# A recurrent block and two feed-forward nets on one core: the second net's down product by columns of tokens, brought back by VectorE and DMAs

## The chip, the core and the metric

The kernel runs on one core of one Trainium2 chip. Time is what the device takes for one execution, in microseconds (us). Before the change the median of three runs is 583.81 us (583.77 to 584.46).

The core has a matrix engine (TensorE, PE in the profile), a vector engine (VectorE, DVE), a scalar engine (ScalarE, ACT), a general engine (GpSimd, POOL) and a queue that here only issues DMAs (SyncE, SP). Each engine runs its own instructions in order and waits on semaphores for the others.

## What is computed

Per batch row of 1024 tokens and 256 features (four rows, so 4096 tokens), in f32, cut to what matters:

```
t   = rmsnorm(x) ;  xb = conv4(t @ Wx) ;  a, i = gates(xb @ Wa, xb @ Wi)
h   = scan(a, sqrt(1 - a*a) * i * xb) ;  h1 = x + (h * gelu(t @ Wy)) @ Wo
u   = rmsnorm(h1)
ffn = (gelu(u @ Wg) * (u @ Wu)) @ Wd                    # first FFN, inner width 1024
x1  = layernorm(x + h1 + ffn)
out = layernorm(x1 + relu(x1 @ W1 + b1) @ W2 + b2)      # second FFN, inner width 1024
```

## The kernel before

**Precision.** Every matrix operand is held as a sum of two rounded parts (`_hi`, `_lo`), and each product is three matmuls: hi by hi, hi by lo, lo by hi. The low parts are made by VectorE (`hidden_lo`, `gate_lo`), the high ones by ScalarE or GpSimd.

**Tiles.** The 4096 tokens are eight chunks of 512 (`CHUNKS`), four tiles of 128 each (`TT`). The inner width of an FFN is eight blocks of 128 (`KH`). A unit is one block of one chunk: 64 units for each FFN.

**Two ways to multiply.** `product` keeps 128x128 of a weight in the array and streams 512 tokens; its sums stand with features on the partitions. `product_by_tokens` keeps 128 tokens in the array and streams 256 columns of a weight; its sums stand with tokens on the partitions, as the row-wise LayerNorm and the output want them. The up products take the first way, both down products the second. A down step is one block of the inner width for one chunk: `down(r)` in the first FFN, `mlp_down(w)` in the second, each four token tiles by three matmuls. The second FFN's down sums of a chunk build up over eight steps in the PSUM banks `SECOND` and `SECOND + 1`.

**Transposes by blocks.** For most chunks a 512x256 matrix is transposed without TensorE: VectorE transposes blocks of 32x32 inside the partitions (STREAM_TRANSPOSE), and DMAs of 32 partitions each carry the blocks to other partitions. `move_x1` does this for x1 with 16 DMAs, `move_t` and `move_u` for t and u with 12 on SyncE's queue and 8 on SyncE's plus 4 on ScalarE's.

**Order.** It is written out by hand. `round_of(r)` on each engine is one round; eight rounds are a period p (m is the round within it). Round r does gate and up of unit r, down of unit r - 1, and in the steady state the up step of unit w = r - 11 of the second FFN and `mlp_down(w - 1)`; the recurrent block of chunk n = p + 1 is spread over rounds 0 to 7. So in period p the first FFN is at chunk p, and chunk s = p - 2 ends its second FFN: its last down step is at the end of round 3. VectorE then adds the sums to the rows at the start of round 4 (`second_sum`), takes statistics at the start of round 6 and normalises in round 7. SyncE's queue is one fixed list: loads, `move_x1`, `move_t`, `move_u`, `store_out`, chunk after chunk. The last chunk's second FFN (`step_up`, `step_down`) is written apart.

**Buffers the change touches.** `normed` holds u for its transpose, later the blocks of x1. `h1[c % 2]` holds h1 of chunk c, and after `add_x_h1` x + h1, until `first_sum(c)` has added it to the first FFN's sums. `rows[c % 2]` holds x1, then x1 + b2, then the output rows.

Of the kernel before, what the change touches and what calls it, by code (L numbers as in the profile page):

```python
# [8 lines left out]
ALU = mybir.AluOpType  # L9
# [19 lines left out]
def griffin_mlp_kernel(nc, x, norm1_w, Wx, Wy, conv_w, conv_b, Wi, Wa, lam, Wo, norm2_w, Wg, Wu, Wd,  # L29
# [14 lines left out]
    with ctx:  # L44
# [3 lines left out]
        def sem(name):  # L48
            return ctx.enter_context(nc.semaphore(name))
# [193 lines left out]
        MOVES = len(ALL_BLOCKS) * DMA  # L243
        OFF_MOVES = len(OFF_DIAGONAL) * DMA

        def by_blocks(c):
            return 1 <= c < CHUNKS - 1

# [37 lines left out]
        tT_done = sem("tT_done")  # L286
        t_blocks_ready = sem("t_blocks_ready")
        t_blocks_moved = sem("t_blocks_moved")
        first_tT_ready = [sem(f"first_tT_ready{q}") for q in range(PAIRS)]
        second_tT_ready = [sem(f"second_tT{k}_ready") for k in range(KD)]  # L290
        half_wx_done = sem("half_wx_done")
# [90 lines left out]
        def _(sync):  # L382
# [27 lines left out]
            def move_x1(c):  # L410
                sync.wait_ge(x1_blocks_ready, KD * c)
                for i, j in ALL_BLOCKS:
                    move_block(sync, flat(normed), flat(gy), x1_blocks_moved, i, j)

            def move_u(c):

                sync.wait_ge(u_blocks_ready, KD * (c - BLOCKWISE + 1))
                for i, j in OFF_DIAGONAL[ACT_MOVES:]:
                    move_block(sync, flat(u_blocks), flat(u_raw), u_blocks_moved, i, j)
# [19 lines left out]
            for c in range(2, CHUNKS):  # L439

                if c == 2:
                    sync.wait_ge(first_xh_ready, PAIRS)
                else:
                    sync.wait_ge(xh_ready, 2 * (c - 2))
                load_x(c)
                if c == 2:
                    sync.wait_ge(lo_split["d"], pieces["d"])
                    load_w("2")
                if c >= 4:
                    move_x1(c - 3)  # L450
                if c >= BLOCKWISE:
                    move_t(c)
                if c >= 4:
                    move_u(c - 1)
                    store_out(c - 4)
            for c in range(CHUNKS - 4, LAST - 1):
                move_x1(c + 1)
                if c + 3 < LAST:
                    move_u(c + 3)
                store_out(c)  # L460
# [11 lines left out]
        def _(pe):  # L472
# [11 lines left out]
            def product_by_tokens(dst, n, k, hi, lo, start, stop):  # L484

                nc.tensor.matmul(dst, hi, w_hi[n][:, k, :], start=start, stop=False, skip_group_check=True)  # L486
                nc.tensor.matmul(dst, hi, w_lo[n][:, k, :], start=False, stop=False, skip_group_check=True)  # L487
                return nc.tensor.matmul(dst, lo, w_hi[n][:, k, :], start=False, stop=stop, skip_group_check=True)  # L488

            def transposed(src, done, bank=MIX):  # L490
                for f in range(KD):
# [23 lines left out]
            def half_bank(bank, tt):  # L515
                return psum[bank + tt // 2][:, (tt % 2) * D:(tt % 2 + 1) * D]

            def toks(tt):
                return slice(tt * P, (tt + 1) * P)
# [264 lines left out]
            def mlp_down(w):  # L784
                c, m = divmod(w, KH)
                pe.wait_ge(hid_lo_ready, w + 1)
                if m == 0 and c >= 1:
                    pe.wait_ge(s2_ready, 2 * c)
                for tt in range(TT):
                    last = product_by_tokens(half_bank(SECOND, tt), "2", m, hid_hi[:, w % SLOTS, toks(tt)],  # L790
                                             hid_lo[:, w % SLOTS, toks(tt)], m == 0 and tt % 2 == 0, m == KH - 1)
                last.then_inc(e_done, 1)

            def units(r):
# [575 lines left out]
        def _(dve):  # L1370
# [182 lines left out]

            def add_mix(c, q, bank=MIX):
                dve.wait_ge(wo_done, 2 * c + q + 1)
                nc.vector.tensor_tensor(pair_of(h1[c % 2], q), psum[bank + q][:, :], pair_of(xs[c % 2], q),
                                        ALU.add).then_inc(h1_ready, 1)

# [27 lines left out]
            def first_sum(c):  # L1586
# [7 lines left out]
                for q in range(PAIRS):  # L1594
                    nc.vector.tensor_tensor(pair_of(rows[c % 2], q), psum[DOWN + q][:, :], pair_of(h1[c % 2], q),
                                            ALU.add).then_inc(s1_ready, 1)

            def second_sum(c):
                dve.wait_ge(e_done, 8 * c + 8)
                dve.wait_ge(b2_added, 4 * c + 4)  # L1600
                for q in range(PAIRS):
                    total = pair_of(rows[c % 2], q)
                    nc.vector.tensor_tensor(total, psum[SECOND + q][:, :], total,
                                            ALU.add).then_inc(s2_ready, 1)

            def gate_times_up(r):
                dve.wait_ge(gelu_ready, r + 1)
# [112 lines left out]
            def round_of(r):  # L1720
# [13 lines left out]
                    if m == 3 and not mixing:  # L1734
                        split_x1_lo(f)
                if m == 4 and second:
                    second_sum(s)
                if m == 5 and mixing and p == 1:
                    scan_both(n)
                if m == (7 if p == 1 else 6) and mixing:  # L1740
# [33 lines left out]
                        hy_lo(n)  # L1774
                if units(r):
                    gate_lo(r)
                if m == 3 and mixing and first and by_blocks(f):
                    split_x1_lo(f)
                if m == 7 and mixing and p >= 2 and n < LAST:
# [143 lines left out]
        def _(pool):  # L1923
# [46 lines left out]
            def norm_u(c):  # L1970
# [5 lines left out]
                if by_blocks(c - 2):  # L1976

                    pool.wait_ge(x1_blocks_moved, MOVES * (c - 2))
                pool.wait_ge(rms2_rstd, h1_squares(c))
                for tt in range(TT):  # L1980
                    nc.gpsimd.tensor_scalar(normed[:, tt, :], h1[c % 2][:, tt, :], rstd2[:, tt:tt + 1], 0.0,
# [158 lines left out]
```

## Time and profile before

| | before |
|---|---|
| median of three runs | 583.81 us |
| profiled execution, its own time | 584.09 us |
| its span (first to last instruction) | 582.3 us |
| TensorE busy | 575.0 us, 99% |
| VectorE busy | 410.3 us, 70% |
| ScalarE busy | 313.9 us, 54% |
| GpSimd busy | 208.5 us, 36% |

A busy matmul is not one that sets the pace: records of neighbouring matmuls overlap, since they are pipelined. What one costs is the distance from its start to the next one's start. One period (69 us) lies between like instructions of neighbouring chunks in the steady state.

### The profile page before, as it was taken

The numbers are of one execution on the slowest core, as the hardware profiler recorded it, in microseconds if no ns is written. First come the engines' busy times: TensorE is split into PE (matmuls) and PEld (weight loads), VectorE is DVE, ScalarE is ACT, GpSimd is POOL, SyncE is SP. The second block draws the span as 40 slices with busy tenths as digits, with TensorE's granted clock in tenths as the row PEclk, the third lists the DMA queues.
The fourth block names the chain that finished last, engine by engine and source line by source line (L and its number), as shares of the span: only waits on it lengthen the run. The fifth ranks groups of instructions, "written<-read, shape, count | busy, mean of one in ns | idle before, by whom it ended". The sixth has DMA issues, their size and how long they took to land.

```text
span 582.3 us, 9342 instructions
## 1 busy us (share of the span) xinstructions
PE 575.0 (99%) x3409; PEld 508.5 (87%) x3409; DVE 410.3 (70%) x737; ACT 313.9 (54%) x600; POOL 208.5 (36%) x318
## 2 busy tenths in 40 slices
PE   8999999999999999999999999999999999999996
PEld 7768888898888988889888988889898898888996
DVE  5889858867747779486885869658795757454665
ACT  6977765844538336483446643575443833232453
POOL 2111335274242543327333354523624043132130
PEclk9999999999999999999999999999999999999999
DMA  7410310011100131002210012100110001100111
GB/s 271 155 37 8 103 36 2 2 27 37 30 7 1 33 95 29 10 1 53 77 37 0 12 43 77 34 1 23 51 33 23 2 1 37 36 1 1 37 37 38
DMA packets 29438, 22.38 MB, mean 38 GB/s; under 512 B 3896, under 2 KB 28624, under 8 KB 29392
## 3 DMA queue, kind: packets, MB, share of 16 engines
q1 hardware_dynamic: 28112, 21.26, 12.0%
q10 hardware_dynamic: 1280, 0.53, 0.4%
q8 instruction: 27, 0.44, 0.3%
q14 instruction: 19, 0.16, 0.1%
HBM read 10.89 MB, written 4.19 MB: 26 GB/s over the span
## 4 chain that ended last, share of the span: by engine, by line
PE 90%; DVE 4%; POOL 2%; ACT 1%; DMA 1%; issue 1%; SPq 1%; DVEq 0%; POOLq 0%; ACTq 0%
PE psum L475 17%; PE psum L477 17%; PE psum L476 17%; PE psum L486 11%; PE psum L488 11%; PE psum L487 11%; PE psum L566 2%; DMA raw_xyai<-in_L_attn_Wi_dram 1%; PE psum L531 1%; PE psum L712 1%; PE psum L714 1%; PE psum L710 1%; DVE gu_lo L1616 1%; PE psum L593 1%; POOL row L2026 0%
## 5 line engine op out<-in xcount | busy, mean ns | idle before, releaser
L2033 POOL TENSOR_SCALAR gu_hi<-gu_raw 128x512 fp32r<-128x512 f32 x64 | 53.9, 842 | 230.3 <-DVE gu_raw L1612 230.2
L1154 ACT ACTIVATE hid_raw<-psum,vecs 128x512 f32<-128x512 f32 x56 | 38.6, 690 | 117.8 <-PE psum L477 117.7
L1612 DVE TENSOR_TENSOR gu_raw<-psum,gu_raw 128x512 f32<-128x512 f32 x64 | 43.8, 685 | 51.6 <-PE psum L477 42.4
L486 PE MATMUL psum<-w_hi,hid_hi 128*128 128x256 f32 x256 | 72.0, 281 | 0.4 <-DVE hid_lo L1621 0.4
L486 PE MATMUL psum<-w_d_hi,gu_hi 128*128 128x256 f32 x256 | 71.9, 281 | 0.0
L488 PE MATMUL psum<-w_hi,hid_lo 128*128 128x256 f32 x256 | 71.9, 281 | 0.0
L488 PE MATMUL psum<-w_d_hi,gu_lo 128*128 128x256 f32 x256 | 71.9, 281 | 0.0
L487 PE MATMUL psum<-w_lo,hid_hi 128*128 128x256 f32 x256 | 71.8, 280 | 0.0
L487 PE MATMUL psum<-w_d_lo,gu_hi 128*128 128x256 f32 x256 | 71.7, 280 | 0.0
L1139 ACT ACTIVATE gu_raw<-psum 128x512 f32<-128x512 f32 x64 | 38.3, 598 | 61.6 <-PE psum L477 36.2
L1616 DVE TENSOR_TENSOR gu_lo<-gu_raw,gu_hi 128x512 fp32r<-128x512 f32 x64 | 47.8, 748 | 24.2 <-POOL gu_hi L2033 24.2
L1621 DVE TENSOR_TENSOR hid_lo<-hid_raw,hid_hi 128x512 fp32r<-128x512 f32 x56 | 41.5, 740 | 32.7 <-ACT hid_hi L1158 32.4
L486 PEld LDWEIGHTS psum<-w_hi,hid_hi 128*128 128x128 f32 x256 | 48.2, 188 | 3.3 <-DVE hid_lo L1621 1.3
L486 PEld LDWEIGHTS psum<-w_d_hi,gu_hi 128*128 128x128 f32 x256 | 48.2, 188 | 3.2 <-DVE gu_lo L1616 0.7
L475 PE MATMUL psum<-uT_hi,w_u_hi 128*128 128x512 f32 x128 | 50.1, 391 | 0.1
L487 PEld LDWEIGHTS psum<-w_d_lo,gu_hi 128*128 128x128 f32 x256 | 48.1, 188 | 2.3
L477 PE MATMUL psum<-uT_hi,w_u_lo 128*128 128x512 f32 x128 | 49.9, 390 | 0.0
L487 PEld LDWEIGHTS psum<-w_lo,hid_hi 128*128 128x128 f32 x256 | 48.1, 188 | 2.1
L476 PE MATMUL psum<-uT_lo,w_u_hi 128*128 128x512 f32 x128 | 49.9, 390 | 0.0
L488 PEld LDWEIGHTS psum<-w_hi,hid_lo 128*128 128x128 f32 x256 | 48.2, 188 | 0.0
L488 PEld LDWEIGHTS psum<-w_d_hi,gu_lo 128*128 128x128 f32 x256 | 48.2, 188 | 0.0
L475 PE MATMUL psum<-uT_hi,w_g_hi 128*128 128x512 f32 x118 | 46.6, 395 | 0.0
(250 smaller groups left out, 1548.2 us busy)
## 6 DMA issues: line engine op xcount, KB each, us to landing
out_dram<-row SPq DMA_DIRECT2D x15, 256.0 KB, 2.2
xs<-in_L_attn_x_dram SPq DMA_DIRECT2D x7, 512.0 KB, 3.5
gy<-normed SPq DMA_DIRECT2D x96, 32.0 KB, 1.9
t_raw<-t_blocks SPq DMA_DIRECT2D x60, 32.0 KB, 1.9
raw_gud<-in_L_attn_Wg_dram SPq DMA_DIRECT2D x1, 1024.0 KB, 9.1
raw_gud<-in_L_attn_Wu_dram SPq DMA_DIRECT2D x1, 1024.0 KB, 11.2
raw_gud<-in_L_attn_Wd_dram SPq DMA_DIRECT2D x1, 1024.0 KB, 13.6
raw_gud<-in_L_ffn_W_dram SPq DMA_DIRECT2D x1, 1024.0 KB, 6.8
```

What stands on the lines that cost most here:

```text
L475: nc.tensor.matmul(dst, w_hi[n][:, k, cols], hi[:, k, :], start=(k == 0), stop=False)
L476: nc.tensor.matmul(dst, w_hi[n][:, k, cols], lo[:, k, :], start=False, stop=False)
L477: return nc.tensor.matmul(dst, w_lo[n][:, k, cols], hi[:, k, :], start=False, stop=(k == KD - 1))
L486: nc.tensor.matmul(dst, hi, w_hi[n][:, k, :], start=start, stop=False, skip_group_check=True)
L487: nc.tensor.matmul(dst, hi, w_lo[n][:, k, :], start=False, stop=False, skip_group_check=True)
L488: return nc.tensor.matmul(dst, lo, w_hi[n][:, k, :], start=False, stop=stop, skip_group_check=True)
L1139: nc.scalar.activation(dst, gate, ACT.Gelu_apprx_tanh).then_inc(gelu_ready, 1)
L1154: nc.scalar.activation(raw, hidden, ACT.Relu, bias=vec("b1", m)).then_inc(relu_ready, 1)
L1612: nc.vector.tensor_tensor(gu, up, gu, ALU.mult).then_inc(gu_ready, 1)
L1616: nc.vector.tensor_tensor(gu_lo[:, r % SLOTS, :], gu_raw[:, r % SLOTS, :], gu_hi[:, r % SLOTS, :].bitcast(FP32), ALU.subtract).then_inc(gu ...
L1621: nc.vector.tensor_tensor(hid_lo[:, w % SLOTS, :], hid_raw[:, w % SLOTS, :], hid_hi[:, w % SLOTS, :].bitcast(FP32), ALU.subtract).then_inc ...
L2033: nc.gpsimd.tensor_scalar(gu_hi[:, r % SLOTS, :], gu_raw[:, r % SLOTS, :], 1.0, 0.0, ALU.mult, ALU.add).then_inc(gu_hi_ready, 1)
```

## The change

The down steps of chunks 0 to 5 of the second FFN now keep 128x128 of W2 in the array and stream 512 tokens: 6 matmuls of 512 columns in place of 12 of 256. The sums then stand with features on the partitions. VectorE's two block transposes (`transpose_e_blocks`) bring them from PSUM into `normed`, sixteen DMAs (`move_e`) carry the blocks to the token rows in the free `h1` buffer, and `second_sum` adds from there, at the end of round 5 and no longer at the start of round 4. Chunks 6 and 7 keep the old way. The PSUM banks are now free for the next chunk after the transposes. New waits guard the buffers: GpSimd's `norm_u` waits for the moves before it writes `normed`, and `add_mix` for the sum before it writes `h1`.

```diff
+        def sum_by_blocks(c):
+            return c < CHUNKS - 2
+        def e_rows(c):
+            return h1[(c + 1) % 2]
...
+            def move_e(c):
+                sync.wait_ge(e_blocks_ready, KD * (c + 1))
+                sync.wait_ge(s1_ready, 2 * (c + 2))
+                blocks = flat(normed).rearrange("p (i g a) -> p i g a", i=GROUPS, a=BLOCK)
+                placed = flat(e_rows(c)).rearrange("p (g j a) -> p g j a", j=GROUPS, a=BLOCK)
+                for i, j in ALL_BLOCKS:
+                    rows_in = slice(j * BLOCK, (j + 1) * BLOCK)
+                    rows_out = slice(i * BLOCK, (i + 1) * BLOCK)
+                    sync.dma_start(placed[rows_out, :, j, :], blocks[rows_in, i, :, :]).then_inc(e_blocks_moved, DMA)
...
                 if c >= 4:
                     move_x1(c - 3)
+                    move_e(c - 4)
                 if c >= BLOCKWISE:
                     move_t(c)
...
             for c in range(CHUNKS - 4, LAST - 1):
                 move_x1(c + 1)
+                move_e(c)
...
+            def product_by_columns(n, m, hi, lo):
+                for f in range(KD):
+                    cols, dst = slice(f * P, (f + 1) * P), psum[SECOND + f][:, :]
+                    nc.tensor.matmul(dst, w_hi[n][:, m, cols], hi, start=(m == 0), stop=False)
+                    nc.tensor.matmul(dst, w_lo[n][:, m, cols], hi, start=False, stop=False)
+                    last = nc.tensor.matmul(dst, w_hi[n][:, m, cols], lo, start=False, stop=(m == KH - 1))
+                return last
...
                 if m == 0 and c >= 1:
-                    pe.wait_ge(s2_ready, 2 * c)
-                for tt in range(TT):
-                    last = product_by_tokens(half_bank(SECOND, tt), "2", m, hid_hi[:, w % SLOTS, toks(tt)],
-                                             hid_lo[:, w % SLOTS, toks(tt)], m == 0 and tt % 2 == 0, m == KH - 1)
+                    pe.wait_ge(e_blocks_ready, KD * c)
+                if sum_by_blocks(c):
+                    last = product_by_columns("2", m, hid_hi[:, w % SLOTS, :], hid_lo[:, w % SLOTS, :])
+                else:
+                    for tt in range(TT):
+                        last = product_by_tokens(...)
...
             def add_mix(c, q, bank=MIX):
                 dve.wait_ge(wo_done, 2 * c + q + 1)
+                if c >= 3:
+                    dve.wait_ge(s2_ready, 2 * (c - 2))
...
+            def transpose_e_blocks(c):
+                dve.wait_ge(e_done, 8 * c + 8)
+                dve.wait_ge(x1_blocks_moved, MOVES * (c + 1))
+                blocks = flat(normed).rearrange("p (i t k a) -> p i t k a", i=GROUPS, t=TT, k=KD)
+                for f in range(KD):
+                    nc.vector.transpose(blocks[:, :, :, f, :],
+                                        psum[SECOND + f][:, :].rearrange("p (t i s) -> p i t s", t=TT, i=GROUPS)
+                                        ).then_inc(e_blocks_ready, 1)
...
             def second_sum(c):
-                dve.wait_ge(e_done, 8 * c + 8)
+                if sum_by_blocks(c):
+                    dve.wait_ge(e_blocks_moved, MOVES * (c + 1))
+                else:
+                    dve.wait_ge(e_done, 8 * c + 8)
                 dve.wait_ge(b2_added, 4 * c + 4)
                 for q in range(PAIRS):
                     total = pair_of(rows[c % 2], q)
-                    nc.vector.tensor_tensor(total, psum[SECOND + q][:, :], total, ALU.add).then_inc(s2_ready, 1)
+                    e = pair_of(e_rows(c), q) if sum_by_blocks(c) else psum[SECOND + q][:, :]
+                    nc.vector.tensor_tensor(total, e, total, ALU.add).then_inc(s2_ready, 1)
...
                 if m == 4 and second:
-                    second_sum(s)
+                    transpose_e_blocks(s)
...
                 if units(r):
                     gate_lo(r)
+                if m == 5 and second:
+                    second_sum(s)
...
+                if c >= 3:
+                    pool.wait_ge(e_blocks_moved, MOVES * (c - 2))
                 pool.wait_ge(rms2_rstd, h1_squares(c))
```

**Where it moves instructions.** On TensorE, one up step of the second FFN (x1T against W1) and the down step behind it (hid against W2), before:

```order
L476 MATMUL psum<-x1T_lo,w_hi 128x512
L477 MATMUL psum<-x1T_hi,w_lo 128x512
L486 MATMUL psum<-w_hi,hid_hi 128x256
L487 MATMUL psum<-w_lo,hid_hi 128x256
L488 MATMUL psum<-w_hi,hid_lo 128x256
```

The same place now:

```order
L499 MATMUL psum<-x1T_lo,w_hi 128x512
L500 MATMUL psum<-x1T_hi,w_lo 128x512
L517 MATMUL psum<-hid_hi,w_hi 128x512
L518 MATMUL psum<-hid_hi,w_lo 128x512
L519 MATMUL psum<-hid_lo,w_hi 128x512
```

The three rows of 256 columns stood four times in a step, the three of 512 stand twice. On VectorE, rounds 4 and 5 of a steady period (row is the output row, gu and hid the two FFNs' inner values, t_blocks the transpose of t, h_1 the h1 buffer), before, shortened in the middle:

```order
L1603 TENSOR_TENSOR row<-psum,row 128x512 x2
L1612 TENSOR_TENSOR gu_raw<-psum,gu_raw 128x512
...
L1612 TENSOR_TENSOR gu_raw<-psum,gu_raw 128x512
L1381 STREAM_TRANSPOSE t_blocks<-t_raw 128x4x4x32 x2
L1616 TENSOR_TENSOR gu_lo<-gu_raw,gu_hi 128x512
L1621 TENSOR_TENSOR hid_lo<-hid_raw,hid_hi 128x512
L1556 TENSOR_TENSOR h_1<-psum,xs 128x512 x2
```

And now:

```order
L1643 STREAM_TRANSPOSE normed<-psum 128x16x32 x2
L1664 TENSOR_TENSOR gu_raw<-psum,gu_raw 128x512
...
L1664 TENSOR_TENSOR gu_raw<-psum,gu_raw 128x512
L1417 STREAM_TRANSPOSE t_blocks<-t_raw 128x4x4x32 x2
L1668 TENSOR_TENSOR gu_lo<-gu_raw,gu_hi 128x512
L1656 TENSOR_TENSOR row<-h_1,row 128x512 x2
L1673 TENSOR_TENSOR hid_lo<-hid_raw,hid_hi 128x512
L1595 TENSOR_TENSOR h_1<-psum,xs 128x512 x2
```

The transposes stand where the sums stood, and the sums stand nearly two rounds later, ahead of `hidden_lo` and `add_mix`. On SyncE's queue, one chunk's transfers, before:

```order
L384 DMA xs<-in_L_attn_x_dram 128x4x256
L236 DMA gy<-normed 32x2x128 x16
L236 DMA t_raw<-t_blocks 32x2x128 x12
L236 DMA u_raw<-u_blocks 32x2x128 x8
L402 DMA out_dram<-row 128x2x256 x2
```

And now:

```order
L394 DMA xs<-in_L_attn_x_dram 128x4x256
L236 DMA gy<-normed 32x2x128 x16
L434 DMA h_1<-normed 32x8x32 x16
L236 DMA t_raw<-t_blocks 32x2x128 x12
L236 DMA u_raw<-u_blocks 32x2x128 x8
L412 DMA out_dram<-row 128x2x256 x2
```

Sixteen DMAs stand ahead of the moves of t and u. Each carries 32 KB like its neighbours, but in 256 runs of 32 floats (128 bytes) where theirs have 64 runs of 128 floats (512 bytes).

## Rows read from the trace of the kernel before

**Rows 1.** The page's head and its row of TensorE: busy us, share, instructions.

```profile
span 582.3 us, 9342 instructions
PE 575.0 (99%) x3409; PEld 508.5 (87%) x3409; DVE 410.3 (70%) x737; ACT 313.9 (54%) x600; POOL 208.5 (36%) x318
```

**Rows 2.** The page's chain of work that ended last, share by engine.

```profile
PE 90%; DVE 4%; POOL 2%; ACT 1%; DMA 1%; issue 1%; SPq 1%; DVEq 0%; POOLq 0%; ACTq 0%
```

**Rows 3.** TensorE's waits: us in all, times, longest.

```profile
PE psum L878 <- POOL ident L2085: 1.5, 1, 1.5
PE psum L486 <- DVE hid_lo L1621: 0.4, 2, 0.2
```

**Rows 4.** One period: busy us of each engine (instructions), granted clock, DMA share, GB/s.

```profile
276.00:345.00 69.00, 69.00 (x409) 61.41 (x408) 50.67 (x89) 36.64 (x69) 29.08 (x45) 1.00 0.13 35
```

**Rows 5.** TensorE in order of time: start, us; first matmuls of neighbouring steps.

```profile
300.39 0.28 PE L486 MATMUL psum<-w_hi,hid_hi 128*128 128x256 f32 x1
...
301.80 0.40 PE L475 MATMUL psum<-uT_hi,w_g_hi 128*128 128x512 f32 x1
...
303.17 0.39 PE L475 MATMUL psum<-uT_hi,w_u_hi 128*128 128x512 f32 x1
...
304.53 0.39 PE L475 MATMUL psum<-mT_hi,w_a_hi 128*128 128x512 f32 x1
```

**Rows 6.** TensorE in order of time, the two waits for hid_lo.

```profile
135.27 0.38 PE L486 MATMUL psum<-w_hi,hid_hi 128*128 128x256 f32 x1 [0.25 <-DVE hid_lo L1621]
...
145.43 0.38 PE L486 MATMUL psum<-w_hi,hid_hi 128*128 128x256 f32 x1 [0.17 <-DVE hid_lo L1621]
```

**Rows 7.** VectorE in order of time, rounds 4 to 6 of period 4.

```profile
314.86 1.28 DVE L1603 TENSOR_TENSOR row<-psum,row 128x512 f32<-128x512 f32 x2
317.16 0.69 DVE L1612 TENSOR_TENSOR gu_raw<-psum,gu_raw 128x512 f32<-128x512 f32 x1 [1.02 <-PE psum L477]
...
329.48 1.29 DVE L1381 STREAM_TRANSPOSE t_blocks<-t_raw 128x512 f32<-128x512 f32 x2
330.70 0.65 DVE L1616 TENSOR_TENSOR gu_lo<-gu_raw,gu_hi 128x512 fp32r<-128x512 f32 x1
...
333.80 0.69 DVE L1556 TENSOR_TENSOR h<-psum,xs 128x512 f32<-128x512 f32 x1 [0.75 <-PE psum L488]
```

**Rows 8.** VectorE in order of time, rounds 4 to 6 of the last period.

```profile
516.83 1.28 DVE L1603 TENSOR_TENSOR row<-psum,row 128x512 f32<-128x512 f32 x2
...
528.60 0.70 DVE L1621 TENSOR_TENSOR hid_lo<-hid_raw,hid_hi 128x512 fp32r<-128x512 f32 x1 [1.89 <-ACT hid_hi L1158]
...
531.51 0.69 DVE L1612 TENSOR_TENSOR gu_raw<-psum,gu_raw 128x512 f32<-128x512 f32 x1 [0.47 <-PE psum L477]
```

**Rows 9.** TensorE in order of time, the last period.

```profile
534.02 0.28 PE L486 MATMUL psum<-w_hi,hid_hi 128*128 128x256 f32 x1
...
535.43 0.40 PE L475 MATMUL psum<-uT_hi,w_g_hi 128*128 128x512 f32 x1
```

**Rows 10.** One move of x1: its issues (ns min/median/max, first and last start), landing.

```profile
L236 SPq DMA_DIRECT2D gy<-normed x16: 592/597/605, 293.6 to 303.1; - x16
...
DMA to landing us min/median/max: 1.8/1.9/3.0
```

**Rows 11.** DMA queues, 293.5 to 305: packets, MB, share of 16 engines.

```profile
q1 hardware_dynamic: 1273, 0.52, 18.6%
```

**Rows 12.** SyncE's queue in order of time, 316 to 346: the next issues.

```profile
330.80 7.62 SPq L236 DMA_DIRECT2D t_raw<-t_blocks  x12
340.31 5.07 SPq L236 DMA_DIRECT2D u_raw<-u_blocks  x8
```

**Rows 13.** The stores' issues: ns min/median/max, first and last start.

```profile
L402 SPq DMA_DIRECT2D out_dram<-row x14: 372/378/400, 212.7 to 564.9; - x14
```

**Rows 14.** The u chain's end: ScalarE, then TensorE, in order of time.

```profile
347.40 1.15 ACT L1012 ACTIVATE uT_hi<-u_raw 128x512 fp32r<-128x512 f32 x2
...
350.18 0.39 PE L645 MATMUL psum<-uT_hi,w_g_hi 128*128 128x512 f32 x1
```

More of the change, by code:

```diff
@@ L288, in griffin_mlp_kernel @@
         t_blocks_moved = sem("t_blocks_moved")
+        e_blocks_ready = sem("e_blocks_ready")
+        e_blocks_moved = sem("e_blocks_moved")
         first_tT_ready = [sem(f"first_tT_ready{q}") for q in range(PAIRS)]
@@ L787, in mlp_down @@
                 if m == 0 and c >= 1:
-                    pe.wait_ge(s2_ready, 2 * c)
-                for tt in range(TT):
-                    last = product_by_tokens(half_bank(SECOND, tt), "2", m, hid_hi[:, w % SLOTS, toks(tt)],
-                                             hid_lo[:, w % SLOTS, toks(tt)], m == 0 and tt % 2 == 0, m == KH - 1)
+                    pe.wait_ge(e_blocks_ready, KD * c)
[3 more added lines that the diff above has]
+                    for tt in range(TT):
+                        last = product_by_tokens(half_bank(SECOND, tt), "2", m, hid_hi[:, w % SLOTS, toks(tt)],
+                                                 hid_lo[:, w % SLOTS, toks(tt)], m == 0 and tt % 2 == 0, m == KH - 1)
                 last.then_inc(e_done, 1)
@@ L1602, in second_sum @@
                     total = pair_of(rows[c % 2], q)
-                    nc.vector.tensor_tensor(total, psum[SECOND + q][:, :], total,
-                                            ALU.add).then_inc(s2_ready, 1)
+                    e = pair_of(e_rows(c), q) if sum_by_blocks(c) else psum[SECOND + q][:, :]
+                    nc.vector.tensor_tensor(total, e, total, ALU.add).then_inc(s2_ready, 1)
             def gate_times_up(r):
```

## The prediction

> **What bounds the kernel now.** I read the page's head first: TensorE is busy 99% of the span [rows 1], and the chain that ended last runs over it for 90% [rows 2]. Busy says little for pipelined matmuls, so the waits come next: TensorE waits 1.5 us once at the start and 0.4 us, in two waits, for `hid_lo`; little else [rows 3]. A whole period shows 69.00 busy of 69.00 us at the full clock (1.00), with VectorE at 50.7, ScalarE at 36.6 and GpSimd at 29.1 us [rows 4]. So between the prologue and the end the time is the sum of the distances between matmul starts. An edit pays by what it takes off that sum, and costs what another engine adds when its slack is gone.
>
> **The down steps.** The 12 matmuls of a down step take from 300.39 to 301.80, 1.41 us or 117.5 ns each; the gate step behind them, 6 matmuls of 512 columns, takes to 303.17, 1.37 us; the up step after that to 304.53, 1.36 us or 227 ns each [rows 5]. The columns are the same, 3072. From 117.5 and 227 follow 109.5 ns for 256 columns and some 8 ns per matmul: six fewer save 0.05 us. A step of 512 columns behind one of 256 costs 0.01 more than one behind its like (1.37 against 1.36), and that goes too. So 1.41 + 1.37 become 1.36 + 1.36: 0.06 us per step.
>
> The Trainium skill, page "TensorE: Matmul & The Clock Gate", section "Wait — 56ns, not 53.3ns?", gives a distance of the columns over 2.4 GHz plus about 2.5 ns. By it a step would go from 12 x 109.2 to 6 x 215.8 ns, 0.015 us less, and the change would bring 0.7 us. The rows show more than three times that fixed part, and the sum goes by the rows.
>
> The step is changed in 6 chunks x 8 = 48 places. Not each counts. The first four down steps of chunk 0 lie in a stretch where TensorE waits for VectorE's `hid_lo` at 135.27 and 145.43 [rows 6]. The first of these is paced by work that began before the down steps ahead of it, so what the first two save becomes a longer wait; the second is paced by VectorE's run from 139.8 on, so the fourth's saving is lost too, while the third's moves that run with it. 45 x 0.06 = **2.7 us**. The bounds are 45 x 0.05 = 2.25 and 48 x 0.06 = 2.9.
>
> **The transposes.** Two on VectorE in place of two sums, in the same place. From PSUM the trace shows none. From SBUF two take 1.29 us (at 329.48) and two sums 1.28 (at 314.86) [rows 7]: nothing changes. At twice that they end 1.3 us later; VectorE idles 1.02 us there before its next instruction, at 317.16 [rows 7], and what is queued behind (`gate_times_up`, then the gates of the recurrence) moves by 0.3 us and meets more idle time. I take nothing. TensorE's wait for the banks comes at the end of round 4, long after.
>
> **The sixteen DMAs.** One move of x1 issues its first at 293.6 and its sixteenth at 303.1: 0.637 us apart; each lands 1.9 us after its issue [rows 10]. The new ones carry the same 32 KB each in four times the runs. Issue: if it grew with the runs it would be 2.4 us each; but the stores, with 256 runs too, take 0.378 us to issue, less than the moves' 0.597 [rows 13, 10]. I take 0.637. Transfer: in 11.5 us the engines spent 18.6% on these packets [rows 11], 0.186 x 16 x 11.5 = 34 us for 16 x 64 = 1024 packets of 512 bytes (the rest are semaphore writes), at most 33 ns each. A new DMA has 256 over 16 engines, 16 on each: 0.53 us at that price, still under 0.637. So the issue sets the pace unless a packet of 128 bytes costs more than one of 512.
>
> In a steady period: transposes done at 316.1 [rows 7], the sixteenth issue 15 x 0.637 = 9.6 us later, landed at 327.6. VectorE reaches the sum after `gate_lo`, at 331.3 [rows 7]. Slack 3.7 us. SyncE's queue is free at 326.3; behind stands `move_t`, which before began at 330.80, when VectorE had its blocks, and then `move_u` at 340.31 [rows 12]: neither moves. GpSimd's `norm_u` waits for the moves too, later still.
>
> **The sum, moved.** Two adds, 1.28 us from PSUM [rows 7] and bounded from SBUF by twice that, now stand at 331.3, ahead of `hidden_lo` and `add_mix`. The second `add_mix` waits for TensorE until 333.80, 0.75 us idle, after 0.2 us idle before the first [rows 7]. So of the 1.2 us some 0.25 stay on the path add_mix, squares, `norm_u`, blocks of u, `move_u`, `uT_hi`; with the sum at double price, 1.5. That path ends on TensorE: `uT_hi` is written twice from 347.40, done by 348.6, and TensorE begins to read the first at 350.18 and the second two matmuls, 0.45 us, later [rows 14]. Slack 2.1 us. It costs nothing; without that cover it would be 0.25 in each of four chunks.
>
> **The last period** has no recurrent work and is shorter, and there the cover fails. Transposes done at 518.1 [rows 8], landed at 518.1 + 9.6 + 1.9 = 529.6, while VectorE is ready for the sum at 526.7 and for `hidden_lo` at 528.60. So VectorE waits some 3 us: sum until 530.8, `hidden_lo` until 531.4, statistics (1.8 us) until 533.3, `gate_times_up` until 533.9; before, it began at 531.51 [rows 8]. TensorE wants `hid_lo` at 534.02 and, for its gate at 535.43, the bank that `gate_times_up` frees [rows 9]; both come some 0.2 us earlier now. Slack 2.4 and 1.25 us. The edge: 1.25 / 15 = 0.08 us more between issues, 0.72 in all, and TensorE waits.
>
> **Sum.** 584.09 - 2.7 = 581.4 for the profiled execution; its span would be 579.6, with the same 1.8 us around it. The profiled execution stands 0.3 above the median of the three, so the median goes from 583.81 to **581.1 us**. This case's own range is 580.9 to 581.6. A measurement tells about 0.2%, 1.2 us, from no change. Chance 0.72.
>
> **Rivals.**
>
> *The blocks come late in the last period only.* With 0.9 us between the new DMAs they land 15 x 0.26 = 3.9 us later; less 1.25 us of slack, TensorE waits 2.7 us, once. In the steady periods the slack of 3.7 nearly covers it. The gain is gone: 583.8. For it: the form 32x8x32 is nowhere in the trace, and the moves already issue slower than the larger stores. Against: 0.53 us of transfer fits under 0.637. 0.08.
>
> *Small packets set the pace, and it ends slower.* If a packet of 128 bytes costs twice one of 512, 67 ns, a DMA holds its engines 1.07 us. The blocks land 15 x 0.43 = 6.5 us later. Last period: 6.5 - 1.25 = 5.2 us of waiting. Steady periods: landed at 334.1, 2.8 us after VectorE is there; `add_mix` and the u chain move by as much, past their 2.1 us: 0.7 us in each of the four chunks whose u goes by blocks, 2.8 us. 583.81 - 2.7 + 5.2 + 2.8 = 589. It decides from 0.9 us per DMA on. Against: 33 ns for 512 bytes leaves 128 bytes little reason to cost more. 0.13, with any slower issue.
>
> The Trainium skill, page "DMA: Bandwidth & Descriptors", speaks for it and against it: "Specifications" wants at least 512 bytes for line rate and has the engine do a read-modify-write below, while "Why small descriptors are slow (HBM only)" says that transfers inside SBUF don't suffer. No row here has packets of 128 bytes.
>
> *The width saves little.* If the 8 ns per matmul belonged to the old steps' operands and the new steps kept all but a third of the saving, 45 x 0.016 = 0.7 us: 583.1. Against: the steps behind them, of 512 columns, show 227 ns each with other operands [rows 5]. 0.04. This is also what the skill's 2.5 ns would give.
>
> What is left, 0.03, is more than I see, on either side.
>
> **The numbers.** Faster by over 0.2% holds the forecast, 0.72, and some of what is left: 0.75. Within 0.2%: late blocks, little width: 0.12. Slower: 0.13. The range reaches below to 48 steps and a little more, 580.7, and above over the late blocks, 584.2; what is left out is mainly the slow packets.
>
> **What would show it.** In the new profile: down steps of chunks 0 to 5 at 1.36 us; a period 0.5 us shorter; new issues 0.64 us apart; idle time before `second_sum` of 3 us once, in the last period, and none before; TensorE's waits as before, with the two for `hid_lo` longer by 0.1 to 0.2 in sum. I am wrong if issues are more than 0.72 apart, if VectorE idles before `second_sum` in the steady periods, if the transposes from PSUM take well over 0.69 each, or if the matmuls of 512 columns on `hid` start more than 227 ns apart.

## The result, and the profile after

The changed kernel takes 585.36 us (median of 11 runs, 585.04 to 587.57) beside 583.99 (11 runs, 583.57 to 584.74) for the kernel before on the same chip: ratio 1.0026, 95% interval [1.0017, 1.0036]. It is slower by 0.26%, where 2.7 us of gain were forecast. The page's head, for [rows 1]:

```profile
span 583.2 us, 8901 instructions
PE 576.0 (99%) x3121; PEld 494.7 (85%) x3121; DVE 417.8 (72%) x749; ACT 313.9 (54%) x600; POOL 211.1 (36%) x318
```

TensorE has 288 matmuls fewer (6 in each of 48 steps) and is busy 1.0 us longer. Its waits, for [rows 3]:

```profile
PE psum L914 <- POOL ident L2142: 1.5, 1, 1.5
PE psum L542 <- ACT normed L1165: 0.3, 1, 0.3
PE psum L517 <- DVE hid_lo L1673: 0.2, 1, 0.2
```

No wait is new. The two waits for `hid_lo`, 0.4 us before, are down to one of 0.2, and one wait of before's profiled execution is gone:

```profile
PE psum L566 <- DMA raw_xyai<-in_L_attn_Wi_dram: 0.4, 1, 0.4
```

That is a load of weights ahead of the steady state, and the traces differ in how long TensorE waits for it (below). So the comparisons between traces start behind it. One stretch of 69 us, for [rows 4]: busy us of each engine, granted clock, DMA share, GB/s.

```profile
276.00:345.00 69.00, 69.00 (x360) 58.92 (x360) 51.91 (x90) 36.27 (x70) 29.74 (x45) 1.00 0.17 43
```

So the clock is full and TensorE idles nowhere: the loss must lie in the distances between matmul starts. The trace of TensorE in order of time, for [rows 5]: the first matmuls of the down step (L517), of the gate, up and first FFN's down steps behind it, and the second and third of the down step.

```profile
322.38 0.40 PE L517 MATMUL psum<-hid_hi,w_hi 128*128 128x512 f32 x1
322.62 0.40 PE L518 MATMUL psum<-hid_hi,w_lo 128*128 128x512 f32 x1
322.85 0.40 PE L519 MATMUL psum<-hid_lo,w_hi 128*128 128x512 f32 x1
...
323.79 0.39 PE L498 MATMUL psum<-uT_hi,w_g_hi 128*128 128x512 f32 x1
...
325.18 0.39 PE L498 MATMUL psum<-uT_hi,w_u_hi 128*128 128x512 f32 x1
...
326.56 0.28 PE L509 MATMUL psum<-w_d_hi,gu_hi 128*128 128x256 f32 x1
```

The down step takes 1.41 us, not 1.36: 235 ns from start to start, not 227. The gate step, whose instructions did not change, takes 1.39, the up step 1.38. Every step of the kind shows it. Below, a step's length is the median start-to-start distance over its occurrences in the steady state (35 to 44 of one kind in each trace): the down step went from 1.410 to 1.409 us, the gate step behind it from 1.368 to 1.392, the up step after that from 1.362 to 1.373. That is +0.034 us where all three follow one another, and less where a step of 256 columns follows. From the first gate matmul of unit 16 to that of unit 60 TensorE takes 1.20 us longer than before.

The rest of the forecast, VectorE for [rows 7]:

```profile
314.81 1.31 DVE L1643 STREAM_TRANSPOSE normed<-psum 128x512 f32<-128x512 f32 x2
317.15 0.69 DVE L1664 TENSOR_TENSOR gu_raw<-psum,gu_raw 128x512 f32<-128x512 f32 x1 [1.03 <-PE psum L500]
...
331.26 1.69 DVE L1656 TENSOR_TENSOR row<-h,row 128x512 f32<-128x512 f32 x2
332.87 0.88 DVE L1673 TENSOR_TENSOR hid_lo<-hid_raw,hid_hi 128x512 fp32r<-128x512 f32 x1
333.67 1.28 DVE L1595 TENSOR_TENSOR h<-psum,xs 128x512 f32<-128x512 f32 x2
```

The transposes from PSUM cost nothing, and VectorE does not wait for the blocks. The new DMAs, for [rows 10, 11]: issue ns min/median/max and landing over all six moves, then the share of the 16 engines in 12 us around one move.

```profile
L434 SPq DMA_DIRECT2D h<-normed x96: 585/611/1483, 177.4 to 528.8; - x96
...
DMA to landing us min/median/max: 1.9/1.9/3.0
```

```profile
DMA packets 4352, 0.53 MB, mean 44 GB/s; under 512 B 4352, under 2 KB 4352, under 8 KB 4352
## 3 DMA queue, kind: packets, MB, share of 16 engines
q1 hardware_dynamic: 4352, 0.53, 26.1%
```

0.261 x 16 x 12 us over 4352 packets is 11.5 ns a packet, the semaphore writes among them counted: less than half of the at most 33 ns of one of 512 bytes. SyncE's queue, for [rows 12]:

```profile
316.15 10.40 SPq L434 DMA_DIRECT2D h<-normed  x16
330.79 7.62 SPq L236 DMA_DIRECT2D t_raw<-t_blocks  x12
341.03 5.07 SPq L236 DMA_DIRECT2D u_raw<-u_blocks  x8
```

The moves of t start where they did, those of u 0.72 us later. VectorE in the last period, for [rows 8]:

```profile
517.14 1.30 DVE L1643 STREAM_TRANSPOSE normed<-psum 128x512 f32<-128x512 f32 x2
...
530.77 1.29 DVE L1656 TENSOR_TENSOR row<-h,row 128x512 f32<-128x512 f32 x2 [3.44 <-DMA h<-normed]
531.98 0.68 DVE L1673 TENSOR_TENSOR hid_lo<-hid_raw,hid_hi 128x512 fp32r<-128x512 f32 x1
...
534.33 0.67 DVE L1664 TENSOR_TENSOR gu_raw<-psum,gu_raw 128x512 f32<-128x512 f32 x1
```

This is the wait of some 3 us that was foreseen, and TensorE does not wait for what follows.

### The profile page after: what moved, and what is told of

The parts are those of the page before. It is cut to its first block, busy times and chain, and to the rows that moved or that the text cites. A ratio compares the mean times of both kernels' runs of the same rounds, so it can differ in the third digit from the quotient of the medians.

```text
span 583.2 us, 8901 instructions
## 1 busy us (share of the span) xinstructions
PE 576.0 (99%) x3121; PEld 494.7 (85%) x3121; DVE 417.8 (72%) x749; ACT 313.9 (54%) x600; POOL 211.1 (36%) x318
## 4 chain that ended last, share of the span: by engine, by line
PE 92%; DVE 4%; POOL 2%; ACT 1%; issue 1%; POOLq 0%; DVEq 0%; ACTq 0%
PE psum L498 17%; PE psum L499 17%; PE psum L500 17%; PE psum L509 7%; PE psum L511 7%; PE psum L510 7%; PE psum L517 4%; PE psum L518 4%; PE psum L519 4%; PE psum L598 2%; PE psum L914 1%; PE psum L563 1%; PE psum L744 1%; PE psum L746 1%; PE psum L742 1%
## 5 line engine op out<-in xcount | busy, mean ns | idle before, releaser
L500 PE MATMUL psum<-uT_hi,w_g_lo 128*128 128x512 f32 x118 | 46.5, 394 | 0.0
L499 PE MATMUL psum<-uT_lo,w_g_hi 128*128 128x512 f32 x118 | 46.4, 393 | 0.0
L498 PE MATMUL psum<-x1T_hi,w_hi 128*128 128x512 f32 x112 | 44.0, 393 | 0.0
L500 PE MATMUL psum<-x1T_hi,w_lo 128*128 128x512 f32 x112 | 43.7, 390 | 0.0
L499 PE MATMUL psum<-x1T_lo,w_hi 128*128 128x512 f32 x112 | 43.6, 390 | 0.0
L517 PE MATMUL psum<-hid_hi,w_hi 128*128 128x512 f32 x96 | 38.3, 399 | 0.4 <-DVE hid_lo L1673 0.2
```

The source lines that it names most:

```text
L498: nc.tensor.matmul(dst, w_hi[n][:, k, cols], hi[:, k, :], start=(k == 0), stop=False)
L499: nc.tensor.matmul(dst, w_hi[n][:, k, cols], lo[:, k, :], start=False, stop=False)
L500: return nc.tensor.matmul(dst, w_lo[n][:, k, cols], hi[:, k, :], start=False, stop=(k == KD - 1))
L517: nc.tensor.matmul(dst, w_hi[n][:, m, cols], hi, start=(m == 0), stop=False)
```

## The experiments

Each run's time is a median beside before on the same chip: 583.65 us for the first four, 583.84, 583.97, 583.75 and 583.91 for the later groups. The diffs are cut to the lines that matter; the kernels built on before also hold `product_by_columns`, as in the change.

### Columns alone, other values, the other FFN

The first question is whether the loss is TensorE's, and whether hid's values (relu leaves zeros) make it. e1 is before with only `mlp_down` changed; the sums stay in the wrong layout, so its output is not the function's:

```diff
+                if c < CHUNKS - 2:
+                    last = product_by_columns("2", m, hid_hi[:, w % SLOTS, :], hid_lo[:, w % SLOTS, :])
+                else:
                     for tt in range(TT):
```

> The kernel before with one edit: the down steps of chunks 0 to 5 of the second FFN stream 512 tokens. No block transposes, no new DMAs, the old sums straight from PSUM, so the output rows of these chunks hold sums in the wrong layout. It separates TensorE's part from all the rest. Theory A (the whole loss lies in TensorE's own matmul distances): 1.2 to 1.5 us slower than before, as the changed kernel; down steps at 1.41 us and the gate step behind at 1.39. Rival (the transposes, DMAs and waits cost the time): about 2.7 us faster than before, 581.2.

584.94 us, ratio 1.0018 [1.001, 1.0027]; steps 1.409 and 1.392 us. From unit 16 to unit 60 it takes 1.21 us longer than before, as the changed kernel does (1.20), with no transposes, moves or moved sum: that loss is in TensorE's own stream. e2 (the changed kernel) and e3 (before) take the zeros away in units 0 to 55, here and in the copy `raw`:

```diff
-                nc.scalar.activation(hi, hidden, ACT.Relu,
+                nc.scalar.activation(hi, hidden, ACT.Identity,
```

> The changed kernel with the ReLU of units 0 to 55 replaced by the identity with the same bias, so that the second FFN's inner values are no longer half exact zeros; the output is no longer the reference's. Theory B (what is slow is a moving operand that is half zeros, through something that depends on the data): the down steps fall from 1.41 to 1.36 us, the gate step behind from 1.39 to 1.36, and the time is 2.5 to 2.9 us below the same edit in the kernel before. Rival C (what is slow is where hid lies, how W2 lies, the banks, or the order of the instructions): nothing moves, 1.41 and 1.39, about 585.3.

> The control for the run beside it: the kernel before with the same ReLU replaced by the identity. Theory B: the old step keeps its 1.41 us, 12 matmuls of 117.5 ns, since zeros stood in the array's stationary side; the time within 0.3 us of before, 584.0. If the data matter on the stationary side too, the distances move here as well, by up to some ns each.

e2: 585.36 us, ratio 1.0026 [1.0016, 1.0036], the same steps. e3: 583.92, 1.0002 [0.9993, 1.0011]. The zeros play no part. e4 changes the first FFN's `down` instead of the second's:

```diff
+                if c < CHUNKS - 2:
+                    last = product_by_columns("d", m, gu_hi[:, r % SLOTS, :], gu_lo[:, r % SLOTS, :], DOWN)
```

> The kernel before with the first FFN's down steps of chunks 0 to 5 streaming 512 tokens (gu against Wd), sums read from PSUM in the wrong layout, as in e1. gu is a product of gelu and up and has next to no zeros. Theory B: steps at 1.36 us, time 2.3 to 2.9 us faster than before, 581.3. Rival D (long runs of 512-column matmuls without the 256-column steps between them are slow, whatever they hold): 1.41 and 1.39 as in e1, 1.2 us slower than before, 585.2.

584.5 us, ratio 1.0014 [1.0005, 1.0022]: down step 1.409 us, the x1T step behind it 1.386 instead of 1.370. The other FFN's tensors, banks and neighbours give the same down step, and a lengthening behind it, 0.016 us where the gate step has 0.024. After this I took it to belong to the form of `product_by_columns`: the order of its three matmuls, its banks or its operands.

### Which operand

Four changes to e1's `product_by_columns` and its call. e5 puts the two matmuls with the same weights next to each other:

```diff
-                    nc.tensor.matmul(dst, w_lo[n][:, m, cols], hi, start=False, stop=False)
-                    last = nc.tensor.matmul(dst, w_hi[n][:, m, cols], lo, start=False, stop=(m == KH - 1))
+                    nc.tensor.matmul(dst, w_hi[n][:, m, cols], lo, start=False, stop=False)
+                    last = nc.tensor.matmul(dst, w_lo[n][:, m, cols], hi, start=False, stop=(m == KH - 1))
```

> The kernel of e1 (before, with the down steps of chunks 0 to 5 by 512 columns), and in these steps the order of the three matmuls is W2 high by hid high, W2 high by hid low, W2 low by hid high, as in the gate and up steps, so that the same weights stand twice in a row. Theory O (the order of the operands, weights changed at every matmul, makes them start 235 ns apart): the down step falls from 1.41 to 1.36 us and the step behind from 1.39 to 1.36, time some 581.5 us beside 583.7 to 584.0 of before. Theories M (where the streamed hid lies), S (where W2 lies) and K (the PSUM bank changes after three matmuls): 1.41 and 1.39, about 584.9 us, as in e1.

e6 streams Wg:

```diff
-                    last = product_by_columns("2", m, hid_hi[:, w % SLOTS, :], hid_lo[:, w % SLOTS, :])
+                    last = product_by_columns("2", m, w_hi["g"][:, 0, 0:T], w_lo["g"][:, 0, 0:T])
```

> The kernel of e1, and the matmuls of these steps stream the first 512 columns of Wg instead of hid (other data in the sum, so the output is not the reference's). Theory M: where or what the streamed tensor is makes the distance; steps at 1.36 and 1.36 us, time some 581.5 us. Theories O, S, K: 1.41 and 1.39, about 584.9 us.

e7 loads W1 (`w_hi["1"][:, m % KD, cols]` and the low part in the three matmuls), e8 has one bank per step (with `start` and `stop` to match):

```diff
-                    cols, dst = slice(f * P, (f + 1) * P), psum[base + f][:, :]
+                    cols, dst = slice(f * P, (f + 1) * P), psum[base + m % KD][:, :]
```

> The kernel of e1, and these steps load blocks of W1 instead of W2 (so the output is not the reference's). Theory S: where the weights lie makes the distance; steps at 1.36 and 1.36 us, time some 581.5 us. Theories O, M, K: 1.41 and 1.39, about 584.9 us.

> The kernel of e1, and all six matmuls of a step add into one PSUM bank, the next step's into the other (the sums of two blocks of features run together, so the output is not the reference's). Theory K: the change of bank after three matmuls makes the distance; steps at 1.36 and 1.36 us, time some 581.5 us. Theories O, M, S: 1.41 and 1.39, about 584.9 us.

e5: 584.95 us, e7: 585.04, e8: 584.81, all with 1.409 and 1.392 to 1.393. e6: 581.11 us, ratio 0.9953 [0.9938, 0.9967] (4 executions). Of the four, only the streamed operand matters. First matmuls of neighbouring steps in e6, TensorE in order of time (x1T, the changed step, gate, up):

```profile
297.62 0.40 PE L475 MATMUL psum<-x1T_hi,w_hi 128*128 128x512 f32 x1
...
298.99 0.39 PE L494 MATMUL psum<-w_g_hi,w_hi 128*128 128x512 f32 x1
...
300.35 0.39 PE L475 MATMUL psum<-uT_hi,w_g_hi 128*128 128x512 f32 x1
...
301.71 0.39 PE L475 MATMUL psum<-uT_hi,w_u_hi 128*128 128x512 f32 x1
```

1.36 and 1.36 us: these are the steps that were forecast. What sets hid (and gu, e4) apart from w, x1T and uT is the place. The kernel lays its tensors out in order, all in multiples of 2048 bytes per partition, but with a gap of 24 floats, `units_gap`, ahead of gu and hid. They start 96 bytes behind a multiple of 4096.

### The place of hid

e9 adds 32 bytes ahead of hid to e1, e10 to the whole changed kernel:

```diff
+        sb("hid_gap", [P, 8])
         hid_raw = sb("hid_raw", [P, SLOTS, T])
```

> The kernel of e1 with 32 bytes of unused room ahead of hid_raw, hid_hi and hid_lo in SBUF. As the tensors are laid out in order, a gap of 96 bytes (units_gap, 24 floats) ahead of gu and hid puts both 96 bytes behind a multiple of 4096 bytes in each partition; w, x1T, uT, tT and mT all start on one. With the 32 bytes hid is 128 behind. Theory L (the place of the streamed tensor: at 96 bytes behind, TensorE streams more slowly): the down step falls from 1.41 to 1.36 us and the step behind from 1.39 to 1.36, time some 581.2 us. Theory N (something else of hid: its values, who writes it and when): 1.41 and 1.39, about 584.9 us, as in e1.

> The changed kernel, whole, with the same 32 bytes ahead of hid. Theory L: steps at 1.36 us, and the time that was predicted for the change, 581.1 to 581.6 us beside 583.6 to 584.0 of before. Theory N: 585.4 us, as the changed kernel.

e11 and e12 take the gap away, in e1 and in before:

```diff
-        sb("units_gap", [P, 24])
```

> The kernel of e1 without units_gap, so that gu and hid start on multiples of 4096 bytes. Theory L: steps at 1.36 us; TensorE gains as in e9. What the gap is for on the other engines is not known from the traces: 581.2 us if nothing, more if reads and writes of gu and hid on ScalarE, VectorE or GpSimd get slower. Theory N: 584.9 us.

> The kernel before, without units_gap: the control of e11. In it gu and hid are never streamed, they are loaded as weights. Theory L: TensorE's steps as before, 1.41, 1.37, 1.36 us, and 583.6 to 584.0 us, if the gap does nothing for the other engines. Should loading 128 tokens of hid or gu as weights also depend on the place, the down steps change from 1.41 us.

e9: 583.66 us (ratio 0.9993 [0.9984, 1.0002]), e10: 584.88 (1.0014 [1.0006, 1.0023]), both with steps of 1.392 and 1.375 us. The place counts, as theory L has it, but 128 bytes behind is not a cure: both numbers of my expectation were too good. That e10 gains less than e9 with the same steps (0.26 us beside 0.78 from unit 16 to unit 60) comes from four late starts, which are told below for e16. e11: 583.89 us (0.9999 [0.999, 1.0008]), with hid's steps at 1.360 and 1.360 us. Its gain is eaten elsewhere, and e12 shows where: 588.18 us, ratio 1.007 [1.0056, 1.0084]. The start of an x1T step, of the down step behind it and of the gate step, in e12:

```profile
300.17 0.40 PE L474 MATMUL psum<-x1T_hi,w_hi 128*128 128x512 f32 x1
...
301.56 0.28 PE L485 MATMUL psum<-w_hi,hid_hi 128*128 128x256 f32 x1
...
302.99 0.40 PE L474 MATMUL psum<-uT_hi,w_g_hi 128*128 128x512 f32 x1
```

Loaded as weights, 128 tokens at a time, hid and gu want the gap: without it a down step takes 1.43 us instead of 1.41 and the step behind 1.39 instead of 1.37. The gap that pays for the old way of multiplying is what the new way stumbles over. And it is this gap that pays, not any: the old down steps of chunk 6, which the other kernels keep, take 1.410 us with hid at 96, 1.432 with hid 512 or 1024 behind (e16, e13), 1.449 at 128 (e9, e10) and 1.430 at 416 (e15).

### Modulo what, and relative to what

e13 (928 bytes ahead of hid, which is then 1024 behind a multiple of 4096) and e16 (416 bytes, 512 behind) are the whole changed kernel; e15 is e1 with 320 bytes. e14 is the changed kernel with W2 laid 96 bytes behind too:

```diff
         sb("units_gap", [P, 24])
+        w_hi["2"] = sb("w_2_hi", [P, W2.shape[0] // P, W2.shape[1]], FP32R)
+        w_lo["2"] = sb("w_2_lo", [P, W2.shape[0] // P, W2.shape[1]], FP32R)
```

> The changed kernel, whole, with 928 bytes of unused room ahead of hid, which then starts 1024 bytes behind a multiple of 4096; gu stays at 96. Theory Q (the place of hid counts modulo 1024 or less): down steps and the steps behind at 1.36 us, some 0.09 us less per step than in the changed kernel, 48 of them: 585.4 - 4.3 = 581.1 us. Were only multiples of 2048 or 4096 good: over 1.36, and 583 to 585 us.

> The changed kernel, whole, with W2's two parts laid behind units_gap, so that W2 too starts 96 bytes behind a multiple of 4096 and hid stays where it is. Theory R (what counts is how the streamed tensor stands to the weights loaded beside it): down steps of chunks 0 to 5 at 1.36 us; those of chunk 6, by tokens, from 1.41 to 1.43; 581.5 us. Theory P (the streamed tensor's place by itself): 1.41 and 1.39 us as in the changed kernel, and in the old-style steps of chunk 6, which stream W2, longer ones too; 585.4 us or a little more.

> The kernel of e1 with 320 bytes ahead of hid, which then starts at 416 modulo 512: W2's blocks, which start on multiples of 512, are then 96 bytes ahead of hid modulo 512, as gu is ahead of Wd in the first FFN's down steps. Theory R: this is the good side; down steps at 1.36 us or less, 581 to 582 us. Theory P: any place off a multiple is bad; 1.38 to 1.41 us, 583.5 to 585 us.

> The changed kernel, whole, with 416 bytes ahead of hid, which then starts 512 bytes behind a multiple of 4096. If the place counts modulo 512 or less: as e13, steps at 1.36 us and 581.1 us. If modulo 1024 only: over 1.36 us and 583 to 585 us, while e13 is at 581.1.

| kernel | hid behind a multiple of 512, bytes | down step, us | step behind, us | time, us |
|---|---|---|---|---|
| changed kernel | 96 | 1.409 | 1.392 | 585.36 |
| e14, W2 at 96 too | 96 | 1.391 | 1.389 | 585.12 |
| e10 | 128 | 1.392 | 1.375 | 584.88 |
| e15 (columns alone) | 416 | 1.403 | 1.392 | 584.82 |
| e16 | 0 | 1.360 | 1.360 | 583.04 |
| e13 | 0 | 1.360 | 1.360 | 583.42 |

The place of the streamed tensor decides: on a multiple of 512 bytes (512 and 1024 behind, and 4096 in e11) the price is gone, at 96, 128 and 416 it is not. A place on an odd multiple of 256 was not tried, so 512 need not be the smallest step that matters. As for the rest, the place of the weights shifts it a little (e14: 0.018 us in the down step) and does not cure it, and the mirrored relation (e15) takes off only 0.006 us. Theory R falls, P and Q hold.

But e13 and e16, whose steps are as forecast, end at ratio 0.9993 [0.9985, 1.0002] and 0.9988 [0.9979, 0.9997], not at 581.1. In e16, TensorE at the second FFN's up step in the last round of a period (the last matmul of the first FFN's down step, then the first two on x1T), and ScalarE ahead of it:

```profile
343.88 0.28 PE L512 MATMUL psum<-w_d_hi,gu_lo 128*128 128x256 f32 x1
344.11 0.50 PE L499 MATMUL psum<-x1T_hi,w_hi 128*128 128x512 f32 x1
344.44 0.40 PE L500 MATMUL psum<-x1T_lo,w_hi 128*128 128x512 f32 x1
```

```profile
340.54 2.80 ACTq L237 DMA_DIRECT2D u_raw<-u_blocks  x4
343.45 0.60 ACT L1176 ACTIVATE gu_raw<-psum 128x512 f32<-128x512 f32 x1 [3.48 <-issue]
```

344.11 is 0.23 us behind a matmul of 256 columns (0.117 is usual), and 344.44 is 0.33 behind one of 512 (0.227 usual): 0.22 us lost at once, 0.26 with what the matmuls behind lose, and as much at 206.28, 275.19 and 413.03. No row of the waits tells of it, since the records of matmuls overlap. `mlp_up` needs the bank that ScalarE's gelu of that round's gate empties at 344.05; the gelu stands behind ScalarE's four transfers of u, and these start when VectorE has u's blocks. In before the gelu starts at 343.23 and TensorE comes at 344.68; in the changed kernel, which has some 0.2 us of room left, at 343.94 and 344.73:

```profile
343.23 0.60 ACT L1139 ACTIVATE gu_raw<-psum 128x512 f32<-128x512 f32 x1 [2.64 <-issue]
```

```profile
343.94 0.60 ACT L1175 ACTIVATE gu_raw<-psum 128x512 f32<-128x512 f32 x1 [3.33 <-issue]
```

### The transfers on ScalarE's queue

e17 is e16 with one change; e18 is e1 with hid 512 behind, so without transposes, moves and moved sum:

```diff
-        ACT_MOVES = 4
+        ACT_MOVES = 3
```

> The changed kernel with hid 512 bytes behind a multiple of 4096 (e16), and ScalarE's queue issues three of the twelve u transfers and SyncE's nine, instead of four and eight. Theory G (ScalarE's gelu, queued behind its u transfers, holds TensorE up 0.24 us once a period in e16): the gelu comes 0.7 us earlier, the four waits go, 583.0 - 1.0 = 582.0 us. The ninth transfer on SyncE's queue brings u 0.6 us later, inside its slack of some 1.4 us. Theory H (the late starts come from something else): 583.0 us, and the late starts stay.

> The kernel of e1 (columns alone; sums taken from PSUM in the wrong layout, no transposes, moves or moved sum) with hid 512 bytes behind a multiple of 4096. Theory G: no late starts; steps 1.36 and 1.36 us; the last two chunks 0.5 us longer than before; 585.0 - 4.3 + 0.5 = 581.2 us, at most 581.6. Theory H: late starts here too, 582.5 to 583 us.

e17: **581.47 us** (581.47 to 582.19, 5 runs), ratio 0.9963 [0.9949, 0.9977]. e18: 581.74, 0.9964 [0.9951, 0.9976]. e17 computes the whole output and beats both kernels. Its page's head, ScalarE, and TensorE at the same place:

```profile
span 579.7 us, 8901 instructions
PE 572.6 (99%) x3121; PEld 495.1 (85%) x3121; DVE 415.7 (72%) x749; ACT 314.1 (54%) x600; POOL 213.6 (37%) x318
```

```profile
339.36 2.15 ACTq L237 DMA_DIRECT2D u_raw<-u_blocks  x3
341.61 0.60 ACT L1176 ACTIVATE gu_raw<-psum 128x512 f32<-128x512 f32 x1 [2.83 <-issue]
```

```profile
342.69 0.28 PE L512 MATMUL psum<-w_d_hi,gu_lo 128*128 128x256 f32 x1
342.81 0.40 PE L499 MATMUL psum<-x1T_hi,w_hi 128*128 128x512 f32 x1
343.04 0.39 PE L500 MATMUL psum<-x1T_lo,w_hi 128*128 128x512 f32 x1
```

The gelu ends 0.6 us before TensorE wants its bank, and the late starts are gone: theory G holds. Against before, TensorE gains 2.64 us from unit 16 to unit 60 in e17 and 1.60 in e16; the difference of 1.04 is the four late starts. The medians differ by 1.57, the fastest executions (582.62 and 581.47) by 1.15. Where the rest of the 1.57 comes from is not known. The profiled execution of e16 is the slowest of its ten (583.85), and its first gate step starts 0.68 us later than that of e17, since it waits for the weights that e17's does not wait for:

```profile
PE psum L599 <- DMA raw_xyai<-in_L_attn_Wi_dram: 0.8, 1, 0.8
```

e10's profiled execution waits 1.1 us there, e13's 0.8 (for VectorE), before's 0.4. Whether this belongs to the kernels or to single executions was not tried. e18's trace has none of the four late starts; it has one of 0.35 us at 510.06, behind the low part of a late x1T. With e18 no faster than e17, the blocks, DMAs and the moved sum cost nothing that these runs can tell, once the queue is mended.

## Why the prediction was wrong

**The step that failed** is the first term of the sum: "1.41 + 1.37 become 1.36 + 1.36: 0.06 us per step". They became 1.409 + 1.392, and the up step behind grew by 0.011. I took the 227 ns of other streamed operands [rows 5] for hid, and only named the doubt at the end ("if the matmuls of 512 columns on `hid` start more than 227 ns apart"). x1T and uT start on multiples of 512 bytes in SBUF, hid 96 bytes behind one. In before nothing streams hid or gu, so its trace could not show the price; the line `units_gap` stood in the code and I did not ask what it was for. With hid on a multiple of 512 the same step gives 1.360 + 1.360, 0.058 us less than before.

**The count of 45 steps** was not tested by itself, but e17 bears it out: from the first gate step to unit 60 TensorE gains 2.61 us where 45 x 0.06 = 2.7 were forecast, and the two waits for `hid_lo` add up to 0.6 us, 0.2 more than before, as foreseen. That its profiled execution has a span of 579.7 us, beside 579.6 forecast, is partly luck: it loses 0.5 us behind unit 60, which the forecast lacks, and it begins its first gate step 0.5 us earlier than before's, which had waited for weights. Its median is 581.47, beside 581.1.

**Transposes at nothing** and **DMAs at 0.637 us apart, landed 1.9 after**: right (0.690 us median from PSUM; 0.65 apart, landed 1.9). The rival of small packets falls: 128 bytes take 11.5 ns, not 67. By the Trainium skill, "DMA: Bandwidth & Descriptors", "Why small descriptors are slow (HBM only)", transfers inside SBUF don't suffer from small pieces, and the trace agrees, with 11.5 ns for 128 bytes and at most 33 for 512; its "Specifications" names a read-modify-write below 512 bytes, and no cost of one shows here.

**The sum, moved**: right in that it cost nothing, wrong in size and in what is late next. The two adds from SBUF take 1.61 us from start to start (331.26 to 332.87), not 1.2, and the chain does not lose 0.25 but 0.72 us: ScalarE squares a pair after each `add_mix`, and the first pair, 1.3 us later than before, drags its squares with it. The nearest cover was not the 2.1 us of `uT_hi` but the 0.85 us of the gelu behind ScalarE's own u transfers (343.83 to 344.68 in before). I had counted the moves of u on SyncE's queue and not those on ScalarE's. In the changed kernel some 0.2 us were left; once TensorE is faster they are gone, and this is worth 1.0 us (e16 beside e17).

**The last period**: right. VectorE waits 3.4 us for the blocks (3 forecast), `gate_times_up` starts at 534.33, and TensorE has no wait.

**The rival that the width saves little** was the nearest in kind, since the new steps kept more than their share; but its cause, something of the old steps' operands, is not it, and it did not foresee that the steps behind get longer.

**What stays open** is why the place counts, and whether 512 bytes are the step of it. The runs show place and effect, not the mechanism. Nor was tried to keep hid at 96 where it is loaded and at 0 where it is streamed. e17 gives back 0.5 us after unit 60, where hid is loaded as before: the old down steps of chunk 6 take 1.433 us instead of 1.410, the steps behind them 1.388 instead of 1.368, and the last chunk's half-size up steps and down steps on hid 0.720 and 0.720 instead of 0.715 and 0.705.

## What to carry to other kernels

A matmul's distance belongs to its form and to where its operands lie: before pricing a step by another's rows, compare the operands' addresses too, and ask what every odd gap in a layout is for. When a tensor changes from being loaded to being streamed, its best place can change with it. When a chain is delayed, follow it into each queue that it feeds, ScalarE's with its compute behind the DMAs included, and take the nearest cover. And when an edit disappoints, look at the steps it did not touch.

## What the runs showed of the hardware

- Streams of 512 float32 columns on TensorE, at a granted clock of 1.00: 227 ns from start to start with the streamed tensor on a multiple of 512 bytes in its partition, 235 ns when 96 bytes behind one (1.409 us for six), 232 ns when 128 behind (1.392), 234 ns when 416 behind (1.403, e15). At 96 behind, the lengthening reaches into the next nine matmuls, on other operands: 1.392 us for the six behind, where they take 1.368 behind an old down step and 1.360 with the streamed tensor on a multiple.
- The other way round for tensors loaded as weights in between streams of 256 columns: 117.5 ns at 96 bytes behind, 119.3 ns on a multiple (1.410 and 1.432 us for twelve), 120.8 ns at 128 behind (1.449, e9). The gap of 96, ahead of gu and hid together, is worth 4.2 us over this kernel (e12).
- The Trainium skill, "TensorE: Matmul & The Clock Gate", section "Wait — 56ns, not 53.3ns?", gives one fixed part of about 2.5 ns per matmul. Here the part above the columns at 2.4 GHz is 13 ns at 512 columns at best, and changes with the operands' place by 8 ns; the measurement decides.
- A DMA inside SBUF in pieces of 128 bytes costs its queue 0.611 us to issue, as one in pieces of 512 bytes does (0.597), and the DMA engines some 11.5 ns a packet, semaphore writes counted in.
